# Routed weights' high halves in the shared stage, joined norm statistics, and a new order of the first routed tiles

## The reference

```python
x = L0_attn_x                                   # 16 x 512 x 128, float32
# block 1: linear recurrence over time
n = layernorm(x)
Bu = einsum('sd,bld->lbs', B, n)                # 64 states
h_t = diag(A) * h_(t-1) + Bu_t
x = x + einsum('ds,lbs->bld', C, h) + D * n
# block 2: one shared expert and one of 8 routed experts for each token
n = layernorm(x)
shared = silu(n @ sg.T) * (n @ su.T) @ sd.T     # 256 hidden
logits = n @ gate_w.T
e, score = argmax(logits), sigmoid(max(logits))
routed = swiglu(n * score, r_gate[e], r_up[e], r_down[e])
x = x + shared + routed
```

## Time and profile before

| | us |
|---|---|
| median of 3 runs | 294.42 (294.12 to 295.4) |
| profiled execution, its own time | 292.25 |
| its span, first to last instruction | 290.2 |
| norm stage, until the first shared matmul | 104.3 |
| shared stage, blocks 0 to 10 | 104.3 to 160.8 |
| until the first routed gate matmul | 165.4 |
| routed stage and last shared blocks, PE | until 280.0 |

### The profile page before, as it was taken

One profiled execution on the slowest core, in us unless ns is written; L12 is line 12 of the kernel. 1 busy time (PEld: TensorE's weight loads), 2 busy tenths in 40 slices (PEclk: granted clock), 3 DMA queues, 4 the chain that ended last, 5 costly groups with the idle time before them and its releaser, 6 DMA issues.

```text
span 290.2 us, 6183 instructions
## 1 busy us (share of the span) xinstructions
PE 237.7 (82%) x1891; PEld 183.1 (63%) x1891; DVE 182.2 (63%) x590; ACT 171.4 (59%) x415; POOL 148.9 (51%) x152
## 2 busy tenths in 40 slices
PE   0695848889789279995999699999999999989950
PEld 0264435556456127673667489999999999756650
DVE  3899996699988855889923145555556665434210
ACT  2835798985987463321344877777767765424420
POOL 1000000007777777777860007777777777776940
PEclk9999995998999759999999789999999999999995
DMA  7999300002222232328527703546456533112993
GB/s 212 397 337 365 109 0 1 2 0 95 101 106 105 103 115 94 115 83 273 210 108 212 236 2 88 164 132 194 135 154 179 144 109 114 49 54 40 160 156 36
DMA packets 25919, 38.36 MB, mean 132 GB/s; under 512 B 3712, under 2 KB 17920, under 8 KB 25328
## 3 DMA queue, kind: packets, MB, share of 16 engines
q1 hardware_dynamic: 15264, 22.03, 24.9%
q0 software_dynamic: 10624, 15.93, 20.7%
HBM read 22.03 MB, written 20.25 MB: 146 GB/s over the span
## 4 chain that ended last, share of the span: by engine, by line
PE 58%; DVE 21%; ACT 12%; issue 4%; DMA 1%; POOL 0%; ACTq 0%
PE bank L446 11%; PE bank L400 9%; PE bank L434 6%; PE bank L436 6%; PE bank L435 6%; PE bank L386 5%; PE bank L387 5%; PE bank L388 5%; ACT n L539 4%; ACT rows L553 3%; PE bank L407 3%; DVE stats L712 3%; DVE stats L681 2%; DVE rows L708 2%; DVE n2T_lo L733 2%
## 5 line engine op out<-in xcount | busy, mean ns | idle before, releaser
L990 POOL DMA_INDIRECT table<-rows,place x64 | 66.1, 1032 | 65.6 <-DVE place L770 46.7
L1031 POOL DMA_INDIRECT out<-w_full x51 | 49.3, 967 | 38.1 <-DVE w_full L966 23.4
L599 ACT ACTIVATE n1T<-bank,g_scale 128x512 f32<-128x512 f32 x32 | 22.0, 687 | 35.4 <-PE bank L388 29.3
L434 PE MATMUL bank<-xT_hi,w_split 128*128 128x256 f16 (+1 forms) x156 | 41.8, 270 | 0.0
L436 PE MATMUL bank<-xT_hi,w_split 128*128 128x256 f16 (+1 forms) x156 | 41.7, 270 | 0.0
L435 PE MATMUL bank<-xT_lo,w_split 128*128 128x256 f16 (+1 forms) x156 | 41.6, 269 | 0.0
L446 PE MATMUL bank<-w_full,hid 128*128 x284 | 38.5, 277 | 0.2
L918 DVE SCALAR_TENSOR_TENSOR hid<-bank,h_scale,n1T 128x512 f32<-128x512 f32 x32 | 23.5, 748 | 24.0 <-ACT n1T L599 21.3
L446 PEld LDWEIGHTS bank<-w_full,hid 128*128 128x128 f32 x284 | 34.8, 192 | 1.4 <-issue 0.4
L400 PEld LDWEIGHTS bank<-w_full,hid 128*128 128x128 f32 x256 | 30.7, 192 | 1.9
L400 PE MATMUL bank<-w_full,hid 128*128 128x128 f32 x256 | 30.9, 275 | 0.0
(11 more groups left out here) (136 smaller groups left out, 444.4 us busy)
## 6 DMA issues: line engine op xcount, KB each, us to landing
w_full<-table SPq DMA_DIRECT2D x24, 264.0 KB, 3.3
rows<-in_x SPq DMA_DIRECT2D x8, 512.0 KB, 8.0
w_full<-in_weights SPq DMA_DIRECT2D x3, 1152.0 KB, 11.7
out<-rows POOLq DMA_DIRECT2D x10, 256.0 KB, 6.6
table<-in_pads SPq DMA_DIRECT2D x1, 2112.0 KB, 8.9
table<-in_pads SPq DMA_DIRECT2D x8, 264.0 KB, 4.0
x_ring<-table SPq DMA_DIRECT2D x8, 264.0 KB, 3.6
table<-rows,place POOLq DMA_INDIRECT x64, 2.4
```

The source lines that it names most:

```text
L434: mm(o, w_of(kind, e, 0, c), xT_hi[k][:, 0:w], start=True, stop=False)
L990: g.indirect_dma_start(table[:, :], bass.IndirectOffsetOnAxis(ap=place[:, i:i + 1], axis=0), rows[:, i, :], None).then_inc(done, 16)
L1031: g.indirect_dma_start(out[:, :], bass.IndirectOffsetOnAxis(ap=x_in[k][:, s, 2 * D:2 * D + 1].bitcast(I32), axis=0), x_in[k][:, s, 0:D], N ...
```

## The change

Four edits. (1) ACT's `weights_hi` is split: the shared expert's halves stay at `s` = 1 and 2, the routed experts' halves (128x2048 each) move to shared blocks `b` = 1 and 2, behind the SiLUs. (2) The eight `bn_aggr` and the negation of each statistics block give way to four instructions over all eight tiles: difference of the two half means, sums of the two halves' three fields, the squared difference times D/4, and their sum; the factor 1/D goes into the square root's scale, and -0.5 into the bias, which becomes a `scalar_tensor_tensor`. (3) `route` writes `one_hot` in the order in which it lies. (4) The first routed tiles get another order on ACT, PE and DVE (`START` = 3).

```diff
+START = 3
@@ tensor engine
             for j in range(TILES):
-                if j + 2 < TILES:
+                if START <= j and j + 2 < TILES:
                     transpose_tile(j + 2)
                 routed_gate_up(j)
                 if j == 0:
                     pe.wait_ge(s_late, MIDDLE)
-                if j >= 2:
+                if 1 <= j < START:
+                    routed_down(j - 1)
+                if j > START:
                     routed_down(j - 2)
+                if j < START:
+                    transpose_tile(j + 2)
@@ scalar engine
-                run(sd1[q % 2][:], mv1[q % 2][:, :, 1], ACT.Sqrt, bias=eps1[:, 0:1]).then_inc(s_sd1, 1)
+                run(sd1[q % 2][:], var1[q % 2][:], ACT.Sqrt, bias=eps1[:, 0:1], scale=1.0 / D).then_inc(s_sd1, 1)
...
+            def routed_weights_hi(k):
+                run(w_split[:, 0, k, 1:EW, :], w_full[:, k, F:].rearrange("p (e f) -> p e f", e=E), ACT.Copy,
+                    scale=w_mul[:, 1 + k:2 + k]).then_inc(s_whi, 1)
...
+                if b in (1, 2):
+                    routed_weights_hi(b - 1)
...
-            act.wait_ge(s_hid, FIRST * FC)
-            act.wait_ge(s_wlo, 4)
             tile_score(0)
             tile_scale(0)
             tile_scale(1)
-            for j in range(-2, TILES):
+            tile_hi(0)
+            tile_score(2)
+            tile_scale(2)
+            tile_hi(1)
+            tile_scale(3)
+            late_base(FIRST - 1)
+            act.wait_ge(s_hid, FIRST * FC)
+            for j in range(TILES):
+                if j < START:
+                    routed_silu(j)
@@ vector engine
-                for t in range(PT):
-                    last = v.bn_aggr(mv1[q % 2][:, t, :], stats1[:, t, :])
-                last.then_inc(s_mv1, 1)
-                dve.wait_ge(s_mv1, q + 1)
-                v.tensor_scalar(minus_mean1[q % 2], mv1[q % 2][:, :, 0], -1.0, None, ALU.mult).then_inc(s_r1, 1)
+                v.tensor_tensor(out=gap1[:], in0=stats1[:, :, 1], in1=stats1[:, :, 4],
+                                op=ALU.subtract).then_inc(s_agg1, 1)
+                v.tensor_tensor(out=sums1[q % 2][:], in0=stats1[:, :, 0:3], in1=stats1[:, :, 3:6],
+                                op=ALU.add).then_inc(s_agg1, 1)
+                dve.wait_ge(s_agg1, 3 * q + 1)
+                v.scalar_tensor_tensor(out=gap_sq1[:], in0=gap1[:], scalar=D / 4.0, in1=gap1[:],
+                                       op0=ALU.mult, op1=ALU.mult).then_inc(s_agg1, 1)
+                dve.wait_ge(s_agg1, 3 * q + 3)
+                v.tensor_tensor(out=var1[q % 2][:], in0=gap_sq1[:], in1=sums1[q % 2][:, :, 2],
+                                op=ALU.add).then_inc(s_var1, 1)
...
-                v.tensor_tensor(out=hot, in0=numbers, in1=first_top[:, :, None].to_broadcast([P, GT, E]),
-                                op=ALU.is_equal).then_inc(s_route, 1)
+                v.tensor_tensor(out=hot, in0=scratch[:, kept["numbers"], None].to_broadcast([P, E, GT]),
+                                in1=first_top[:, None, :].to_broadcast([P, E, GT]), op=ALU.is_equal).then_inc(s_route, 1)
...
-            for j in range(-2, TILES):
+            tile_lo(0)
+            tile_lo(1)
+            for j in range(START):
+                routed_hidden(j)
+                if j >= 1:
+                    routed_result(j - 1)
+                tile_lo(j + 2)
+            for j in range(START, TILES):
```

More of the change, by code:

```diff
@@ L123, in block_kernel @@
         stats1 = sb("stats1", [P, PT, 6])
-        mv1 = [sb(f"mv1_{k}", [P, PT, 2]) for k in range(2)]
+        sums1 = [sb(f"sums1_{k}", [P, PT, 3]) for k in range(2)]
+        gap1 = sb("gap1", [P, PT])
+        gap_sq1 = sb("gap_sq1", [P, PT])
+        var1 = [sb(f"var1_{k}", [P, PT]) for k in range(2)]
         sd1 = [sb(f"sd1_{k}", [P, PT]) for k in range(2)]
@@ L131, in block_kernel @@
         stats2 = sb("stats2", [P, PT, 6])
-        mv2 = [sb(f"mv2_{k}", [P, PT, 2]) for k in range(2)]
+        sums2 = [sb(f"sums2_{k}", [P, PT, 3]) for k in range(2)]
+        gap2 = sb("gap2", [P, PT])
+        gap_sq2 = sb("gap_sq2", [P, PT])
+        var2 = [sb(f"var2_{k}", [P, PT]) for k in range(2)]
         sd2 = [sb(f"sd2_{k}", [P, PT]) for k in range(2)]
@@ L525, in std1 @@
             def std1(q):
-                act.wait_ge(s_mv1, q + 1)
-                after(act, s_r1, 2 * (q - 1))
-                run(sd1[q % 2][:], mv1[q % 2][:, :, 1], ACT.Sqrt, bias=eps1[:, 0:1]).then_inc(s_sd1, 1)
+                act.wait_ge(s_var1, q + 1)
+                after(act, s_r1, q - 1)
+                run(sd1[q % 2][:], var1[q % 2][:], ACT.Sqrt, bias=eps1[:, 0:1], scale=1.0 / D).then_inc(s_sd1, 1)
             def std2(q):
-                act.wait_ge(s_mv2, q + 1)
-                after(act, s_r2, 2 * (q - 1))
-                run(sd2[q % 2][:], mv2[q % 2][:, :, 1], ACT.Sqrt, bias=eps2[:, 0:1], scale=X_SCALE ** -2).then_inc(s_sd2, 1)
+                act.wait_ge(s_var2, q + 1)
+                after(act, s_r2, q - 1)
+                run(sd2[q % 2][:], var2[q % 2][:], ACT.Sqrt, bias=eps2[:, 0:1],
+                    scale=X_SCALE ** -2 / D).then_inc(s_sd2, 1)
             def norm1(q):
@@ L565, in router_hi, with shared_weights_hi @@
                 run(router_split[:, 0, :], router_f, ACT.Copy, scale=w_mul[:, 0:1]).then_inc(s_rhi, 1)
-            def weights_hi(k):
+            def shared_weights_hi(k):
                 act.wait_ge(s_scale, 2)
-                full = w_full[:, k, :].rearrange("p (e f) -> p e f", e=EW)
-                for experts in (slice(0, 1), slice(1, EW)):
-                    run(w_split[:, 0, k, experts, :], full[:, experts], ACT.Copy, scale=w_mul[:, 1 + k:2 + k]).then_inc(s_whi, 1)
+                run(w_split[:, 0, k, 0, :], w_full[:, k, 0:F], ACT.Copy, scale=w_mul[:, 1 + k:2 + k]).then_inc(s_whi, 1)
+            def routed_weights_hi(k):
+                run(w_split[:, 0, k, 1:EW, :], w_full[:, k, F:].rearrange("p (e f) -> p e f", e=E), ACT.Copy,
+                    scale=w_mul[:, 1 + k:2 + k]).then_inc(s_whi, 1)
             act.wait_ge(s_eps, 3)
@@ L639, in routed_silu @@
                 run(silu[j % 2][:, 0:w], gate_bank[j % 2][:, 0:w], ACT.Silu, scale=g_scale[:, 0:1]).then_inc(r_silu, 1)
[L641 to L644 removed]
+            for b in range(FIRST):
+                shared_silu(b * FC, 0)
+                shared_silu(b * FC + 1, 1)
                 if b == 0:
```

51 lines of the change are left out of this document (26 added, 25 removed).

## The result

The changed kernel takes 285.91 us (median of four runs, 285.48 to 286.02); the kernel before takes 294.63 (four runs, 294.12 to 295.4). The ratio is 0.970, with a 95% interval of 0.9675 to 0.9724: 8.7 us faster. Forecast were 284.6 us and a range of 281.8 to 288.8. The two profiled executions, 285.48 and 292.25 us, lie only 6.8 us apart. That difference of 1.9 us is the subject of half the experiments. Ratios are made without the executions that lie over 1.5% above the fastest of their kernel.

A forecast was written before the change was run, and what follows sets the result against it. Limits differ by stage: ACT, then DVE in the norm stage, PE in the shared and routed stages. Gains of 6.75 there and 3.1 at the routed start sum to 9.85, from the median 294.42 to 284.6 us; range 281.8 to 288.8.

The forecast's parts named there:

- Statistics and `one_hot`: DVE's norm blocks and `route`: 0.28 us gained per statistics block (16 blocks), 0.41 us per `route` from writing in order.
- Round by round through the norm stage: Norm stage, gains followed pair by pair: 0.62 at pair 0, 3.08 at pair 3, 6.75 us at the first shared matmul.
- the middle of 4.4: Second norm of pair 3: gain taken between 3.3 us if the clock falls and 5.4 if it stays up.
- Copies: ACT's routed high-half copies, twice 1.90 us, go into shared-stage gaps with 1.7 and 0.9 us left; nothing comes back.
- The norm stage's gain is absorbed: Rival, norm stage: PE's chain to `y` holds the loop, only one copy counts; 6.4 us gained, 288.0 us; chance 0.08.
- Shared stage, gain unchanged: Shared stage: PE-bound, elsewhere DVE's `tile_map` moves along, so the 6.75 us gain stays if POOL keeps up.
- first gate matmul 9 to 10 us earlier: Sign to check at the start of the routed stage: first routed gate matmul 9 to 10 us earlier than 165.4.
- Start of the routed stage: First routed tiles in the new order: gate matmul 2.9 us earlier, third down 2.4 to 3.7 us earlier, taken as 3.1.
- "up" case: Start of the routed stage with PE's clock staying up: third down begins at 172.9, a gain of 3.7 us.
- The median: Whole kernel: the runs' median, 294.42 us, lies 2.2 us above the profiled execution; forecast made from the median, 284.6.
- Tile loads, routed pace, end: Routed stage: loads have cover enough, PE keeps 2.4 us per 256-row tile, last additions wait for ACT and so PE.
- slower: Rival, routed start: PE's brief stops keep the clock low, 4.8 us per tile instead of 2.4; six make 299; chance 0.03.

The follow-up runs named there:

- e9: The changed kernel, unedited, run again on a chip where the kernel before takes 339.4 us; ratio to the kernel before 0.9704 (0.9659 to 0.9748), 10.0 us less.
- e2: Kernel before with only the routed weights' high-half copies moved into the shared stage; ratio to the kernel before 0.9822 (0.9713 to 0.993), 6.0 us less.
- e6: Kernel before with 14 added, unused 128x512 matmuls on PE in the wait for `tile_map`; ratio to the kernel before 0.9927 (0.9891 to 0.9963), 2.5 us less.
- e11: Changed kernel with 14 added, unused 128x512 matmuls on PE in the wait for `tile_map`; ratio to the kernel before 0.9673 (0.9633 to 0.9713).
- e5: The kernel before, unedited, run again for another profiled execution; ratio to the other runs of the kernel before 0.9982 (0.9946 to 1.0018).

## Why the prediction came out as it did

**Statistics and `one_hot`: right.** 0.49 us a block against 0.48, and 0.29 for the write in order. The Trainium skill, "VectorE: DVE Perf Modes", section "The DRAIN you can't avoid", as the prediction quotes it would have given 0.68 a block, and that is not what the trace shows. The section also says, and the prediction leaves out, that a next instruction that isn't held starts earlier; read whole, it doesn't speak against the trace.

**Round by round through the norm stage: right, with one term that another offset.** The forecast took the DMA of pair 1 as it had landed before. It landed 1.3 us later, and the first gains were 0.02 and 2.39 instead of 0.62 and 3.08. In e9, where it landed earlier, they are 0.60 (24.81) and 3.03 (38.35). Yet both are 4.46 early at the second norm of pair 3: after starts late and keeps its clock (`bu` 1.94 us), e9 starts early and loses it (2.81). So the middle of 4.4 was luck in part: the two executions differ in two things that offset each other. The clock's price was too high as well. The prediction had 3.3 with the clock down and 5.4 with it up (its own terms, 3.3 + 0.7 + 1.0, give 5.0); from the first norm of pair 3 to the second after gains 2.07 and e9 1.43, only 0.64 apart. And the 3.23 us of wait that it blamed for the low clock aren't the condition: e9 falls behind 1.04 and 0.88 us, after stays up behind 1.33 and 0.88. From pair 3 on each step comes as forecast: 5.36 at pairs 4 and 5, 6.03 at pair 6 (forecast 6.1), 6.54 at the first shared matmul (6.75). The Trainium skill, "TensorE: Matmul & The Clock Gate", section "What's actually happening", says that the moment of the change of clock varies from run to run; the two traces of one kernel agree.

**Copies: right.** They went under PE, with 1.79 and 0.96 us left. "The norm stage's gain is absorbed" is refuted by e2, which has 2.39 us at the first norm of pair 3 and 4.46 at the second.

**"Shared stage, gain unchanged": the step that failed.** The prediction said that DVE's `tile_map` moves along and took PE's stretch behind it as the trace of before showed it, with the clock at 1.00. It priced the clock at two other places and not at this one, though PE waits there 3.5 us in one piece, longer than the 3.23 us that it blamed at pair 3. The changed kernel's profiled execution fell there and lost 2.62 us; 0.55 more went in the first shared block, whose clock the prediction didn't price either. The check "first gate matmul 9 to 10 us earlier" failed for these two: 6.13 and 3.16 are 9.29. The forecast's number held all the same, since it was taken from a median that seems to carry the same fall already (below); the prediction didn't know that, so at this step it is luck.

**Start of the routed stage: the mechanism right, the value in the "up" case.** Clock up was priced at 3.7 for the third down, down at 2.4, taken 3.1; measured 3.88 with the clock at 1.00 (before, the third down starts at 176.74, not at the 176.6 that the prediction read). A middle was the wrong thing to take: with the new order all seven traces are up. The first gate matmul came 2.75 us earlier relative to the stage, forecast 2.9.

**The median.** The terms that hold sum to 6.54 + 3.88 = 10.4, the medians give 8.7, the profiled pair 6.8. The prediction took the 2.2 us between the profiled execution and the median of before as a constant that would come on top. It fits the price of the fall under `tile_map` (1.6 to 2.8 us in the traces, 2.5 by e6's ratio): the profiled execution of before had escaped it, and the changed kernel's profiled execution, which didn't, lies 0.4 us under its own median. The runs behind the medians have no trace by place, so this is an inference. The only thing on record is the mean granted clock of the changed kernel's four runs: 0.952 in the profiled one, 0.934 to 0.941 in the others, which are 0.4 to 0.5 us longer. If both medians carry the fall, 10.4 should show in them. 0.1 is lost by the last addition and 0.4 behind it, and 0.55 would be the first shared block's clock; the other 0.7 us stay open.

**Tile loads, routed pace, end: right.** No wait for a load at the first scores, granted clock 1.00 in the routed stage, additions released by ACT. The rival "slower" had the clock low for six tiles; it was low for none. The chances add up to 0.91 for faster and 0.06 for the same, not to the 0.92 and 0.05 stated.

## What to carry to other kernels

Work on a full engine that has cover in a later stage is worth its own time when moved: 3.8 us of copies gave 3.7 to 6.0, with wide intervals. Before taking a stretch as unchanged, look at every wait of TensorE in it, and price both levels of the clock behind it; here falls came behind waits of 0.4 to 1.0 us as well as behind 3.5. An order that closes TensorE's holes can settle the level, as the new routed start does in seven traces of seven. And when one execution is the basis, ask which of its stretches would differ in the next: a profile 2 us below its own median probably has a stretch that the other executions don't, and a forecast from the median shouldn't count that stretch as the profile shows it.

## What was not expected of the hardware

The same program on one chip loses the clock behind waits of TensorE of 1.04 and 0.88 us in one execution (e9) and keeps it at 1.00 behind 1.33 and 0.88 us in another (e11). Behind a wait of 3.45 to 4.29 us the clock was at 0.50 in eight traces, behind 3.46 and 2.60 at 1.00, and 14 useless matmuls in that wait made the kernel before 2.5 us faster.

On the chips of the experiments the same program takes 339.4 instead of 294.6 us with the same durations of single instructions. Part of the difference at least is stalls like these, in PE's timeline of e5, between matmuls of one group that wait for no other engine:

```profile
72.37 0.17 PE L352 MATMUL bank<-router_split,n2T_hi 128*128 128x8 f16 x1
73.82 0.17 PE L353 MATMUL bank<-router_split,n2T_hi 128*128 128x8 f16 x1 [1.28 <-issue]
75.26 0.17 PE L354 MATMUL bank<-router_split,n2T_lo 128*128 128x8 f16 x1 [1.28 <-issue]
```

"issue" is 11.5% of the chain that ended last in e5 and 4% before. What the engine waits for there, no view shows, and no experiment was made on it.
